# Second attention of a two-layer transformer block: both halves of the scores at the head of a round

## The chip, the core and the metric

The kernel runs on one core of a Trainium2 chip. The metric is the device time of one execution in microseconds (us). Before the change three timed executions gave 514.21, 514.8 and 516.99 us; the median is 514.8 us.

## The reference

The input `x` holds 16 sequences of 128 tokens with 128 features, `ctx_768` holds 16 contexts of 128 rows with 96 features. Four layers follow each other, each added to its own input:

```python
x = x + L0_xattn(layernorm(x), ctx)    # 16 heads of 8, softmax over 128 keys
x = x + L0_ffn(layernorm(x))           # 8 experts, the two best of each token
x = x + L1_xattn(layernorm(x), ctx)    # 16 heads of 64
x = x + L1_ffn(layernorm(x))           # 16 experts, each takes its 32 best tokens
```

The change lies in the third layer, which is

```python
q = split(x @ Wq + lora(x))                             # 16 heads of 64
k, v = split(ctx[:124] @ Wk + ...), split(ctx[:124] @ Wv + ...)
k2, v2 = split(ctx[124:] @ Wk_ipa), split(ctx[124:] @ Wv_ipa)   # the last 4 rows
out = softmax(q k^T / 8) v + softmax(q k2^T / 8) v2
return out @ Wo + bo + lora(out)
```

## The kernel before

All of the work is written out for each engine by hand. An engine takes its instructions in the order of its program, and semaphores, counted up by the engine that makes a value and waited on by the one that takes it, join the engines. Nothing is rearranged by a scheduler. So what sets the order is the text of the five functions called `round1` (one for each of TensorE, VectorE, ScalarE and GpSimd, and weights on SyncE).

The second attention runs in rounds, from -1 to 16. In round `b` the scores and the softmax of sequence `b` are made, while the probabilities of `t = b - 1` are turned and multiplied with the values, and the queries, keys and values of `f = b + 1` are made. A part of the first feed-forward layer, that of sequence `g = b + 4`, runs between them. All 16 heads of one sequence are held at once. Their scores lie in four of the eight banks of PSUM, banks 0 to 3, four heads in each, and banks 4 to 7 serve all the rest in turns.

TensorE's program in an ordinary round `b`, with short names used below:

- S0 is `scores(b, 0)` (L1510), which fills banks 0 and 1, and S1 is `scores(b, 1)`, which fills banks 2 and 3.
- T0 to T3 are `turn(t, n)` (L1521), four transposes each.
- Q0 and Q1 are `queries(f, n)` (L1530), F0 and F1 are the two halves of `ffn(g, ...)` (L1463), both in bank 7.
- K0 and K1 are `keys` (L1538), O0 and O1 are `outputs(t, n)` (L1551), V0 and V1 are `values` (L1558), `inputs` (L1564) turns one tile, and P is the projection (L1721).

The order is S0, T0, Q0, T1, Q1, F0, S1, T2, K0, T3, F1, O0, O1, K1, V0, `inputs`, V1, P. The waits that matter here: Q1 uses the bank of T0 and waits until T0's result is copied, K0 waits likewise for T1's copy, T2 waits for ScalarE's copy of Q0, F1 waits for ScalarE's `weighted` (L1111, F0's result times the expert's weight). O1 reads the copies of T2 and T3 and uses T3's bank, so it waits for T3's copy. S1 waits for the second half of the keys, `Z.k1_sb`, of its own sequence, for which V1 of the round before has waited already.

VectorE's program in round `b`: M0 (`shifted(b, 0)`, L772, L773, L775: the maxima of bank 0), C0 (`turned(t, 0)`, L783: the copy of T0), M1, C1, one reciprocal (L789), then small jobs that differ from round to round (statistics in every round up to 12, parts of the choice of experts in rounds 1 to 8, of the later router in 13 and 14), then M2, C2, M3, a copy of K0 (L919), C3, `weighted` (L745), three reciprocals and the small softmax of the four extra keys. It ends with the residual (L306), which waits for P. In round 15 other copies (`turned` on ScalarE, L1173) and one-hot tiles (`onehot`, L872) for the last layer's gather (L1609 on TensorE, told what to fetch by L1601) come in between.

ScalarE's program in round `b`: the exponentials (`powers`, L1150) of bank 0, the copy of Q0 (L1157), the exponentials of bank 1, the copy of Q1, `weighted` (L1111, four instructions), the exponentials of banks 2 and 3, then copies of O0, K1, O1, the turned tile, V0 and V1. Exponentials of bank `n` wait for M`n`.

The waits of the scores and of the turns, in the code before:

```python
def scores(b, half):
    pe.wait_ge(Z.q_sb, 2 * b + half + 1)
    pe.wait_ge((Z.k0_sb, Z.k1_sb)[half], b + 1)
    pe.wait_ge(Z.ki, b + 1)
    after(pe, Z.exp, CH * (b - 1) + 2 * half + 2)
...
queries(f, 1, *((Z.p_sb, CH * t + 1) if there(t) else (Z.q_sb, 2 * f)))
...
outputs(t, 1, *p_copied(t, 3))
```

Of the kernel before, what the change touches and what calls it, by code (L numbers as in the profile page):

```python
# [37 lines left out]
def after(eng, sem, value):  # L38

    if not isinstance(value, int) or value >= 1:  # L40
        eng.wait_ge(sem, value)


def there(b):
    return not isinstance(b, int) or 0 <= b < B
# [6 lines left out]
def build_program(nc, T, out):  # L52

    with ExitStack() as ctx:
# [15 lines left out]
        def blocks(b_, rows=128):  # L70
            return b_[0:rows, :].rearrange("p (g n) -> p g n", g=CH)
# [1256 lines left out]
        def _(pe):  # L1328
# [132 lines left out]
            def ffn(g, half, to):  # L1461

                pe.matmul(blocks(to), xT0[:, g % 8, :], we[:, 4 * half:4 * half + 4, :], start=True, stop=True)\  # L1463
                    .then_inc((F.ya, F.yb)[half], 1)
# [36 lines left out]
# [6 lines that stand above are left out]
                for c in range(CH):  # L1507
                    for odd in range(2):
                        rows = slice(D1 * odd, D1 * odd + D1)
                        mm = pe.matmul(blocks(bank[2 * half + odd])[:, c, :], q1T[rows, b % 2, CH * half + c, :],  # L1510
                                       k1T[rows, b % 2, CH * half + c, :], start=True, stop=True)
                        if c == CH - 1:
                            mm.then_inc(Z.score, 1)

            def turn(t, n, freed, count):

                pe.wait_ge(Z.norm, CH * t + n + 1)
                pe.wait_ge(Z.ipa_p, t + 1)
                after(pe, freed, count)
                for c in range(CH):  # L1520
                    mm = pe.transpose(blocks(bank[(4, 6, 5, 4)[n]])[:, c, :], p1[:, t % 2, n, c, :], ident[:, :])  # L1521
                mm.then_inc(Z.turned, 1)
# [89 lines left out]
            def round1(b):  # L1612
# [3 lines left out]
                    pe.wait_ge(W.added, ALL_ADDED)  # L1616
                if there(b):
                    scores(b, 0)
                if there(t):
                    turn(t, 0, Z.o_sb, 2 * t)  # L1620
                if b == B:
# [26 lines left out]
                if there(g):  # L1648
                    if j:
                        pe.wait_ge(F.step, HEAD_STEPS * j + 1)  # L1650
                    ffn(g, 0, bank[7])
                if there(b):
                    scores(b, 1)
                if there(t):
                    turn(t, 2, *((Z.q_sb, 2 * f + 1) if there(f) else (Z.v_sb, 2 * B - 1)))
                if b == B:
# [125 lines left out]
            for b in range(-1, B + 1):  # L1782
                round1(b)
# [95 lines left out]
```

## Time and profile before

| what | value |
|---|---|
| median of the timed executions | 514.8 us |
| span of the profiled execution, first to last instruction | 513.1 us |
| TensorE busy | 487.3 us, 95% |
| VectorE busy | 354.2 us, 69% |
| ScalarE busy | 288.2 us, 56% |
| GpSimd busy | 234.4 us, 46% |
| second attention, rounds 0 to 16 | about 135 to 393 us |

The profile gives no other time for the profiled execution than its span. The median lies 1.7 us above it.

The table of rounds is read from the timeline of TensorE and VectorE, in us. A round begins where S0 begins on TensorE. "C0" is the start of VectorE's first copy, counted from the round's start. "J" is the time of the small jobs: from the reciprocal behind C1 until the last small job has given way to the next instruction, without the wait for S1 behind it.

| round | begins | length | C0 | J |
|---|---|---|---|---|
| 1 | 146.56 | 16.81 | 3.04 | 1.95 |
| 2 | 163.37 | 15.25 | 1.94 | 2.03 |
| 3 | 178.62 | 15.61 | 1.95 | 2.49 |
| 4 | 194.23 | 15.68 | 2.47 | 1.96 |
| 5 | 209.91 | 16.64 | 2.41 | 1.96 |
| 6 | 226.55 | 15.26 | 1.95 | 2.03 |
| 7 | 241.81 | 15.60 | 1.94 | 2.49 |
| 8 | 257.41 | 15.23 | 1.95 | 1.96 |
| 9 | 272.64 | 15.24 | 1.95 | 0.67 |
| 10 | 287.88 | 15.61 | 2.39 | 0.68 |
| 11 | 303.49 | 16.29 | 3.08 | 0.67 |
| 12 | 319.78 | 17.68 | 3.07 | 0.66 |
| 13 | 337.46 | 16.16 | 1.95 | 0.68 |
| 14 | 353.62 | 14.35 | 1.94 | 1.18 |
| 15 | 367.97 | 14.84 | 2.13 | |

Rounds 12 and later have no F0 and F1. Rounds 1 and 5 carry two more steps of TensorE, 12 and 13 the router's. In a profile an instruction's row has its start, its duration, engine, line, operation, output and input, and how many it stands for. The duration of a pipelined matmul includes its end, so that the next one can begin before it is over. In brackets stands how long the engine was idle before it, and who ended that.

### The profile page before, as it was taken

The page shows a single profiled execution, that of the slowest core. Times are in us where ns is not written, and L with a number is a line of the kernel's source. Part 1 is how long each engine was busy: PE and PEld are TensorE (multiplying, and loading weights), DVE is VectorE, ACT ScalarE, POOL GpSimd, SP SyncE. Part 2 cuts the span into 40 slices and gives each one's busy share as a digit, 9 for nine tenths or more (in the row PEclk, how much of TensorE's full clock was granted, in tenths as well). Part 3 has the DMA queues.
Part 4 walks back from the last instruction along what each step waited for, and adds up shares of the span by engine and source line. Part 5 has one row for each costly group of instructions (what it writes and reads, how often), then busy time and mean ns, then how long its engine had stood idle before and what let it go on. Part 6 is the DMA issues. An engine that isn't in the chain of part 4 may idle for free.

```text
span 513.1 us, 13570 instructions
## 1 busy us (share of the span) xinstructions
PE 487.3 (95%) x5109; PEld 378.7 (74%) x5113; DVE 354.2 (69%) x1000; ACT 288.2 (56%) x984; POOL 234.4 (46%) x331
## 2 busy tenths in 40 slices
PE   4799999998999999999999999899999999999996
PEld 3466766656668778887787777788757897799995
DVE  5888989766786678566786665757866588535553
ACT  3366566463586776666867657665664444413332
POOL 4845545035365544575444755324231980090440
PEclk9699999999999999999999999999999999999999
DMA  8900000000001100111000000022202100000001
GB/s 229 234 3 4 3 3 3 3 1 8 4 1 32 34 20 16 34 33 34 3 2 2 4 3 3 1 66 64 64 0 71 56 0 1 1 22 24 1 2 42
DMA packets 21872, 14.48 MB, mean 28 GB/s; under 512 B 5928, under 2 KB 21136, under 8 KB 21808
## 3 DMA queue, kind: packets, MB, share of 16 engines
q1 hardware_dynamic: 20704, 13.31, 9.6%
q8 instruction: 42, 0.69, 0.6%
q10 hardware_dynamic: 1104, 0.30, 0.3%
q14 instruction: 22, 0.18, 0.1%
HBM read 12.30 MB, written 1.05 MB: 26 GB/s over the span
## 4 chain that ended last, share of the span: by engine, by line
PE 79%; DVE 12%; ACT 3%; issue 2%; DMA 1%; POOL 1%; ACTq 0%; DVEq 0%; POOLq 0%
PE bank L1792 9%; PE bank L1721 6%; PE bank L1551 5%; PE bank L1558 5%; PE bank L1801 5%; PE bank L1538 5%; PE bank L1510 5%; PE bank L1374 5%; PE bank L1463 5%; PE bank L1521 4%; PE bank L1530 4%; PE bank L1808 3%; PE bank L1609 3%; PE bank L1359 3%; ACT work L1150 2%
## 5 line engine op out<-in xcount | busy, mean ns | idle before, releaser
L1150 ACT ACTIVATE work<-bank,negmax 128x124 f32<-128x124 f32 x256 | 90.0, 387 | 52.2 <-DVE ipa_s L775 52.0
L498 POOL TENSOR_TENSOR work<-work,rsum 128x496 f32<-128x496 f32 x64 | 64.1, 1012 | 120.2 <-DVE rsum L789 120.2
L533 POOL TENSOR_SCALAR work<-work,slot 128x128 f32<-128x128 f32 x64 | 49.7, 792 | 48.3 <-DVE slot L864 29.4
L1150 ACT ACTIVATION_READ_ACCUMULATOR work<-bank,negmax 128x1 f32 x256 | 58.9, 230 | 0.0
L1792 PE MATMUL bank<-work 128*128 128x256 f32 x224 | 53.4, 381 | 0.0
L1014 DVE SCALAR_TENSOR_TENSOR work<-work,bank 128x256 f32<-128x256 f32 x64 | 26.9, 421 | 33.0 <-ACT work L1302 32.8
L1302 ACT ACTIVATE work<-bank 128x256 f32<-128x256 f32 x64 | 24.5, 383 | 40.6 <-PE bank L1792 29.1
L481 POOL TENSOR_TENSOR work<-work 128x512 f32<-128x512 f32 (+2 forms) x48 | 39.2, 817 | 12.1 <-DVE work L745 9.6
L306 DVE TENSOR_TENSOR x_all<-bank,x_all 128x128 f32<-128x128 f32 x16 | 4.7, 292 | 57.4 <-PE bank L1721 55.4
L1792 PEld LDWEIGHTS bank<-work 128*128 128x128 f32 x224 | 40.3, 190 | 4.7 <-DVE work L1017 0.2
L773 DVE TENSOR_REDUCE negmax<-bank 128x4 f32<-128x496 f32 x64 | 42.5, 664 | 0.0
L432 POOL TENSOR_TENSOR rstd<-veps,minus_half 128x1 f32<-128x1 f32 (+3 forms) x28 | 21.2, 755 | 46.1 <-DVE veps L575 45.8
L783 DVE COPY work<-bank 128x512 f32<-128x512 f32 x60 | 40.9, 681 | 0.8 <-PE bank L1521 0.8
L1510 PEld LDWEIGHTS bank<-work 64*128 64x128 f32 x512 | 31.1, 187 | 13.9 <-ACT work L1157 7.6
L629 DVE TENSOR_REDUCE negmax<-bank 128x8 bf16<-128x1024 f32 x32 | 39.1, 1221 | 2.2 <-PE bank L1344 1.7
L1521 PE MATMUL bank<-ident,work 128*128 128x128 f32 x256 | 40.1, 279 | 0.1
L1510 PE MATMUL bank<-work 64*128 64x128 f32 x512 | 37.2, 285 | 1.1 <-issue 1.1
L1090 ACT ACTIVATE work<-bank 128x1024 f32<-128x1024 f32 x32 | 31.0, 1021 | 11.8 <-PE bank L1359 11.8
L1551 PEld LDWEIGHTS bank<-work 128*64 128x64 f32 x512 | 27.7, 136 | 13.5 <-issue 8.7
L1721 PEld LDWEIGHTS bank<-work 128*128 128x128 f32 x256 | 31.1, 192 | 7.4 <-ACT work L1163 5.4
L1530 PE MATMUL bank<-xT,work 128*128 128x128 f32 x256 | 34.3, 278 | 1.6 <-DVE work L783 1.4
L1538 PE MATMUL bank<-cT_all,work 96*128 96x124 f32 x256 | 35.1, 280 | 0.0
(197 smaller groups left out, 1101.1 us busy)
## 6 DMA issues: line engine op xcount, KB each, us to landing
work<-in_L_ffn_w_dram SPq DMA_DIRECT2D x42, 128.0 KB, 2.3
x_all<-in_x_dram SPq DMA_DIRECT2D x4, 256.0 KB, 5.8
out_dram<-x_all SPq DMA_DIRECT2D x4, 256.0 KB, 2.6
ctx_all<-in_ctx_dram SPq DMA_DIRECT2D x4, 192.0 KB, 6.0
ctx_all<-in_L_ffn_w_dram SPq DMA_DIRECT2D x6, 128.0 KB, 2.3
work<-in_L_xattn_Wq_dram SPq DMA_DIRECT2D x1, 512.0 KB, 6.5
work<-in_L_xattn_Wo_dram SPq DMA_DIRECT2D x1, 512.0 KB, 8.2
work<-in_L_ffn_We_dram SPq DMA_DIRECT2D x1, 512.0 KB, 5.7
```

The lines of the kernel that those rows point to most:

```text
L498: pool.tensor_tensor(part, part, rsum1[:, b % 2, CH * n:CH * n + CH].unsqueeze(2).broadcast_to((128, CH, ORG)), ALU.mult).then_inc(Z.norm, 1)
L533: ins = pool.tensor_scalar(ohw_of(e)[:, k, :], count[:, :], slot[:, h, 0, k, e % E1:e % E1 + 1], slot[:, h, 1, k, e % E1:e % E1 + 1], ALU. ...
L773: dve.tensor_reduce(negmax1[:, b % 2, part], got_s[:, :, 0:ORG], X, ALU.max, negate=True)
L783: dve.tensor_copy(p1T[:, CH * n:CH * n + CH, :], blocks(bank[(4, 6, 5, 4)[n]])).then_inc(Z.p_sb, 1)
L1150: ins = act.activation(p1[:, b % 2, n, c, 0:ORG], blocks(bank[n])[:, c, 0:ORG], ACT.Exp, bias=negmax1[:, b % 2, h:h + 1], accum_out=sums1[ ...
L1510: mm = pe.matmul(blocks(bank[2 * half + odd])[:, c, :], q1T[rows, b % 2, CH * half + c, :], k1T[rows, b % 2, CH * half + c, :], start=True ...
L1521: mm = pe.transpose(blocks(bank[(4, 6, 5, 4)[n]])[:, c, :], p1[:, t % 2, n, c, :], ident[:, :])
L1530: mm = pe.matmul(blocks(bank[5 - n])[:, c, :], wq1[:, part], xT[:, f % 2, :], start=True, stop=True)
L1538: mm = pe.matmul(bank[6][:, ORG * c:ORG * c + ORG], wk1[0:C, part], cT_all[:, f, 0:ORG], start=True, stop=True)
L1551: mm = pe.matmul(blocks(bank[5 - n])[D1 * odd:D1 * odd + D1, c, :], v1[:, t % 2, D1 * h:D1 * h + D1], p1T[:, CH * (2 * n + odd) + c, :], s ...
L1721: mm = pe.matmul(bank[7][:, 0:D], o1T[:, c, :], wo1[:, c, :], start=(c == 0), stop=(c == 7))
L1792: mm = pe.matmul(halves(bank[4 + c])[:, n, :], up_weights(e, n, c), xgT[e // E1][:, :, e % E1, :], start=True, stop=True)
```

## The change

One call moves. `scores(b, 1)` is called directly behind `scores(b, 0)`, at the head of TensorE's round, and no longer between `ffn(g, 0)` and `turn(t, 2)`. The work, the banks, the semaphores and the waits within the call are the same. The programs of all other engines are unchanged.

```diff
                 if there(b):
                     scores(b, 0)
+                    scores(b, 1)
                 if there(t):
                     turn(t, 0, Z.o_sb, 2 * t)
...
                     ffn(g, 0, bank[7])
-                if there(b):
-                    scores(b, 1)
                 if there(t):
                     turn(t, 2, *((Z.q_sb, 2 * f + 1) if there(f) else (Z.v_sb, 2 * B - 1)))
```

An ordinary round on TensorE, round 2, from P of the round before (L1721) to O0 and O1. Before:

```order
251 L1721 MATMUL bank<-work 128x128 x8
252 L1510 MATMUL bank<-work 128x128 x8
253 L1521 MATMUL bank<-ident,work 128x128 x4
254 L1530 MATMUL bank<-xT,work 128x128 x4
255 L1521 MATMUL bank<-ident,work 128x128 x4
256 L1530 MATMUL bank<-xT,work 128x128 x4
257 L1463 MATMUL bank<-work 128x512
258 L1510 MATMUL bank<-work 128x128 x8
259 L1521 MATMUL bank<-ident,work 128x128 x4
260 L1538 MATMUL bank<-cT_all,work 128x124 x4
261 L1521 MATMUL bank<-ident,work 128x128 x4
262 L1463 MATMUL bank<-work 128x512
```

The same place after the change (L1721 is L1720 there):

```order
249 L1720 MATMUL bank<-work 128x128 x8
250 L1510 MATMUL bank<-work 128x128 x16
251 L1521 MATMUL bank<-ident,work 128x128 x4
252 L1530 MATMUL bank<-xT,work 128x128 x4
253 L1521 MATMUL bank<-ident,work 128x128 x4
254 L1530 MATMUL bank<-xT,work 128x128 x4
255 L1463 MATMUL bank<-work 128x512
256 L1521 MATMUL bank<-ident,work 128x128 x4
257 L1538 MATMUL bank<-cT_all,work 128x124 x4
258 L1521 MATMUL bank<-ident,work 128x128 x4
259 L1463 MATMUL bank<-work 128x512
```

T0, Q0, T1, Q1 and F0 come eight matmuls later, and everything from T2 on has the same work ahead of it as before.

VectorE's order from C1 of round 2 to M2 and C2, which is the same in both kernels (L310 to L575 are the statistics, L714 and L715 compare the experts):

```order
265 L783 COPY work<-bank 128x512
266 L789 RECIPROCAL rsum<-sums 128x4
267 L310 BN_STATS stats<-x_all 128x6
268 L572 BN_AGGR mv<-stats 128x2
269 L575 TENSOR_SCALAR veps<-mv 128x1
270 L714 TENSOR_TENSOR work<-work 128x256
271 L715 TENSOR_TENSOR work<-work,lower 128x256
272 L772 TENSOR_REDUCE ipa_max<-bank 128x4
273 L773 TENSOR_REDUCE negmax<-bank 128x4
274 L775 TENSOR_TENSOR ipa_s<-bank,ipa_max 128x16
275 L783 COPY work<-bank 128x512
```

Nothing moved there: VectorE still takes the scores of bank 2 only behind both copies and the small jobs.

## Rows read from the trace of the kernel before

**Rows 1.** Waits of TensorE in rounds 2 to 12: total, times, longest.

```profile
PE bank L1551 <- DVE work L783: 1.4, 4, 0.8
PE bank L1530 <- DVE work L783: 1.4, 3, 0.8
```

**Rows 2.** Timeline of TensorE, round 6: start, duration, engine, line, operation, tiles, count.

```profile
226.55 1.16 PE L1510 MATMUL bank<-work 64*128 64x128 f32 x16
227.64 0.66 PE L1521 MATMUL bank<-ident,work 128*128 128x128 f32 x4
...
229.47 1.06 PE L1530 MATMUL bank<-xT,work 128*128 128x128 f32 x8
...
231.31 1.16 PE L1510 MATMUL bank<-work 64*128 64x128 f32 x16
...
234.23 1.02 PE L1463 MATMUL bank<-work 128*128 128x512 f32 x2
235.18 1.99 PE L1551 MATMUL bank<-work 128*64 128x128 f32 x32
237.10 1.16 PE L1538 MATMUL bank<-cT_all,work 96*128 96x124 f32 x8
...
241.81 1.16 PE L1510 MATMUL bank<-work 64*128 64x128 f32 x16
```

**Rows 3.** Timeline of VectorE, round 6.

```profile
227.74 0.17 DVE L772 TENSOR_REDUCE ipa_max<-bank 128x4 f32<-128x16 f32 x1 [0.22 <-PE bank L1510]
...
228.50 0.68 DVE L783 COPY work<-bank 128x512 f32<-128x512 f32 x1
...
230.44 0.17 DVE L789 RECIPROCAL rsum<-sums 128x4 f32<-128x4 f32 x1
...
232.57 0.17 DVE L772 TENSOR_REDUCE ipa_max<-bank 128x4 f32<-128x16 f32 x1
...
235.25 0.68 DVE L783 COPY work<-bank 128x512 f32<-128x512 f32 x1
```

**Rows 4.** Timeline of VectorE, round 3: its first and its last copy.

```profile
180.57 0.68 DVE L783 COPY work<-bank 128x512 f32<-128x512 f32 x1
...
187.67 0.68 DVE L783 COPY work<-bank 128x512 f32<-128x512 f32 x1
```

**Rows 5.** Timeline of TensorE: waits in rounds 0, 3, 11, 14 and 15.

```profile
142.13 1.13 PE L1463 MATMUL bank<-work 128*128 128x512 f32 x2 [0.79 <-ACT work L1111]
...
188.50 1.09 PE L1551 MATMUL bank<-work 128*64 128x128 f32 x16 [0.15 <-DVE work L783]
...
307.39 1.13 PE L1530 MATMUL bank<-xT,work 128*128 128x128 f32 x8 [0.82 <-DVE work L783]
...
362.28 1.09 PE L1551 MATMUL bank<-work 128*64 128x128 f32 x16 [0.66 <-DVE work L783]
...
372.24 1.12 PE L1609 MATMUL bank<-work 128*128 128x512 f32 x2 [0.19 <-DVE work L872]
```

**Rows 6.** Timeline of VectorE, rounds 12, 14 (first and last copy) and 15.

```profile
327.99 0.68 DVE L814 SCALAR_TENSOR_TENSOR work<-work,bank 128x512 f32<-128x512 f32 x1
...
355.56 0.68 DVE L783 COPY work<-bank 128x512 f32<-128x512 f32 x1
...
361.45 0.68 DVE L783 COPY work<-bank 128x512 f32<-128x512 f32 x1
...
370.10 0.68 DVE L783 COPY work<-bank 128x512 f32<-128x512 f32 x1
...
371.44 0.75 DVE L872 TENSOR_SCALAR work<-bank,tok 128x512 f32<-128x512 f32 x1
```

**Rows 7.** Timeline of ScalarE, rounds 0 and 11 (`weighted`) and 12 (the router's tanh).

```profile
140.88 1.20 ACT L1111 ACTIVATE work<-bank,work 128x128 f32<-128x128 f32 x4
...
310.36 1.20 ACT L1111 ACTIVATE work<-bank,work 128x128 f32<-128x128 f32 x4
...
327.12 0.66 ACT L1190 ACTIVATE work<-bank 128x512 f32<-128x512 f32 x1
```

## The prediction

> **What bounds the kernel now.** I read the page's busy shares first: TensorE has matmuls in 95% of the span, no other engine over 69%. The time is therefore TensorE's work and the few holes in it. The move adds and removes no instruction, so only the holes can change. In the waits of TensorE over rounds 2 to 12 [rows 1] there are two that count, both for VectorE's copy L783: the outputs (O1) and the queries (Q1), 1.4 us each. VectorE is thus the engine whose schedule matters, although it is busy for 69% only. Next come the timelines of one round. Round 6 on TensorE [rows 2] runs from 226.55 to 241.81 without a hole, 15.26 us, and S1 starts 4.76 us into it. VectorE in the same round [rows 3] shows the state before the change: M0 begins at 227.74, as soon as S0 is over (226.55 + 1.16), C0 follows at 228.50 without a wait since T0 was over by 228.30, and M2 at 232.57 comes just behind the small jobs and S1's end (232.47).
>
> **What moves.** S0 takes 1.09 us of TensorE before T0 can start [rows 2], and S1 as much. With S1 in front, T0, Q0, T1, Q1 and F0 start 1.09 us later, while T2 and all behind it start as before, the round being as long. No wait of S1 holds it at the head: V1 of the round before has waited for the same keys, and the exponentials of bank 3 are over in the middle of that round. What changes is when VectorE gets its inputs. M0 is unchanged. T0 now starts 2.18 us into a round and is over 0.66 us later; with the 0.03 us from S0's end to M0, C0 can start no earlier than 2.87. Before, it started at 1.94 or 1.95 in rounds 2, 3, 6, 7, 8, 9, 13 and 14 (table of rounds), directly behind M0. VectorE now stands still for 0.92 us there, with M1 behind the copy in its queue although S0 has filled bank 1. M2 in turn can start earlier, since S1 is over at 2.28.
>
> **The rule for one round.** In round 3 C3 started 7.10 us after C0 [rows 4], of which the small jobs J are 2.49; the rest, 4.61, is six pieces of M and C and the copy of K0 at their usual pace. O1 started 0.83 us after C3 [rows 5], 188.50 against 187.67. So afterwards O1 can start no earlier than 2.87 + 4.61 + J + 0.83 = 8.31 + J. TensorE itself is ready for O1 at 9.59 us (O0 starts 8.63 into round 6, and half of the 1.92 until K1 is the first half) [rows 2]. A round stays free of a hole while J is at most 1.28 us. T1's copy needs no more: T1 is over at 2.87 + 1.33, just when M1 is. A round with a hole is 0.07 us longer than the hole itself: round 3 started O1 0.29 late and was 0.36 longer than 15.25.
>
> **Rounds that lose**, J from the table of rounds:
> - 2 and 6, J 2.03: O1 at 10.34, 0.75 late, with 0.07 it is 0.82 each, 1.64 together. They had no hole, but only 0.06 us to spare: C3 at 235.25 plus 0.83 is 236.08, O1 could start at 236.14 [rows 2, 3].
> - 3 and 7, J 2.49: O1 at 10.80, 1.21 late, 1.28 longer than an empty round against 0.36 before: 0.92 each, 1.84 together.
> - 8, J 1.96: O1 at 10.27, 0.68 late: 0.75.
> - 4, J 1.96: the same 0.75, but the round had already lost 0.43 at Q1 (15.68 against 15.25), which goes. Net 0.32.
> - 14, no feed-forward step, so TensorE comes to O1 1.9 us earlier and is waiting already: O1 at 8.66 [rows 5], C3 at 361.45 [rows 6]. Now 8.31 + 1.18 = 9.49: 0.83.
> - 15: C0 started 2.13 in [rows 6], now 2.87. The one-hot tile at 371.44 is queued behind M1, and the gather at 372.24 waited for it [rows 5]. ScalarE's exponentials of bank 1 wait for the same M1, and the next `tell` for ScalarE's copy behind them. Both arms shift by the same 0.74, and I take it in full; if ScalarE's arm had room the round would lose less, down to 0.
>
> Sum of the losses: 1.64 + 1.84 + 0.75 + 0.32 + 0.83 + 0.74 = 6.12 us.
>
> **Rounds that gain.** Where VectorE came late into the round, C0 held Q1 up. Q1 now starts 1.09 us later by itself, at 4.01, and C0, which was later than or near 2.87 anyhow, no longer holds it.
> - 10: 0.36 (15.61 to 15.25).
> - 11: C0 at 3.08, the hole before Q1 at 307.39 [rows 5] made the round 16.29 long. All of 1.04 would go, but then ScalarE is late: its `weighted` starts at 310.36 and F1 can follow 1.25 us behind its start (round 0: 142.13 after 140.88) [rows 5, 7]. That is 311.61, 8.12 into the round, where TensorE is ready for F1 at 7.68 [rows 2]. A hole of 0.44 + 0.07 stays: gain 0.53.
> - 12: VectorE would be earlier by the 1.70 us that it waited for S1, but its product L814 at 327.99 [rows 6] needs the tanh, which ScalarE has at 327.12 + 0.66 = 327.78 [rows 7], with all ScalarE's work before it unmoved. C3 comes 0.18 earlier: gain 0.18.
> - 1: F0 waited some 0.16 us for a copy of the expert's logits, which now has room: gain 0.16, an estimate from the length of that round.
>
> Sum of the gains: 0.36 + 0.53 + 0.18 + 0.16 = 1.23 us.
>
> **Rounds at nothing.** 0 has no turns and its holes are ScalarE's, whose order is the same. 9 has J 0.67, far under 1.28. 5 gets its logits 1.09 later on VectorE, and O1 would wait for C3 until 10.9 where TensorE is ready at 11.0: covered by 0.1, and worth up to 0.3 if not. 13 has 0.7 to spare before O0. In an ordinary round ScalarE's `weighted` starts some 0.45 later since Q0 and M1 are; that leaves F1 about 0.2 us. GpSimd's normalisation moves by at most 0.9 us, and it stood still for 5 us a round.
>
> **The sum.** 6.12 - 1.23 = 4.89 us. The profiled execution's span of 513.1 becomes 518.0; the median lies 1.7 us higher, at 514.8, so it becomes **519.7 us**, 0.95% more.
>
> **A page that says otherwise.** Rows 1 show TensorE, the busiest engine, waiting for VectorE's copies at two places. The Trainium skill, Perfetto Trace Analysis, Optimization Strategy, says to look for the gaps on the most contended engine and to make the things it waits for start sooner or finish faster. Taken by that rule the change is right: the scores for half of VectorE's maxima are there some 3 us before VectorE comes to them. It would change the sum from a loss to the gain of the first rival below. The trace speaks against it, for M2's wait was not what made C3 late; in the crowded rounds M2 had followed the small jobs at once.
>
> **Rivals.**
> - *The earlier scores pay, faster.* VectorE takes M2 up to 1.3 us sooner, and all the holes at L783 close. For it: rounds 9 to 12 show M2 waiting for S1 for over a microsecond. The price is the 1.4 + 1.4 us of rows 1 and some 0.07 for each of seven, 3.3 us: 511.5. It decides at J below 1.28 with C0 not delayed, and eight rounds of the table are above. 5%.
> - *C0's wait is absorbed, no change.* The copy could be held less than 0.92 us, or the pieces between C0 and C3 could run closer together once bank 2 is ready. If only the gains come and round 15's shift vanishes, it is 514.8 - 1.2 = 513.6; that takes all of O1's slack from somewhere the rows don't show. 7%.
> - *Half of it.* Round 15's and 14's shifts hidden by ScalarE, and 0.2 us less in each of rounds 2 to 8: 4.9 - 1.5 - 1.2 = 2.2, 517.0. 15%.
> - *ScalarE becomes late too.* If `weighted` is later by 0.5 more than I find, F1 waits about 0.3 us in rounds 1, 5, 9, 10 and 11, where O1 doesn't cover it, and round 5's 0.1 of cover goes: 4.9 + 1.8 = 6.7, 521.5. For it: 0.2 us is all the room there is. 13%.
> - *The forecast*: 60%.
>
> **The numbers.** The forecast alone spans about 518.3 to 521.0, from seven terms of some 0.1 each and round 15. The half case lies at 517.0 and ScalarE's at 521.5; the range of 516.6 to 522.0 takes in both and leaves out the two first rivals and some tails, under 2 in 10. A measurement of this kernel can tell about 0.5% from no change, 2.6 us here. Slower by more: the forecast, ScalarE's case and a third of the half case, 0.78. Within: 0.17. Faster: 0.05.
>
> **What the profile afterwards would show.** If right: TensorE's busy time unchanged; C0 with an idle time of about 0.9 us before it, ended by TensorE's L1521, in rounds 2, 3, 6, 7, 8, 9 and 14; M2 without any wait for L1510 in any round; TensorE's wait for L783 at L1551 in rounds 2 to 12 up from 1.4 us to about 5, at Q1 gone; rounds 2 and 6 at 16.07, 3 and 7 at 16.53, 8 and 4 at 16.0, 9 at 15.24, 10 at 15.25. It is wrong if C0 follows M0 at once, if C3 in round 2 starts earlier than 9.3 us into the round, if F1 waits for L1111 in ordinary rounds, or if holes appear at the head of a round, before S1.

## The result and the profile after

The changed kernel takes 518.55 us, the median of 15 executions, against 516.17 us for the kernel before in as many on the same chips. The ratio is 1.0046, with a 95% interval from 1.003 to 1.0061: about 2.4 us slower, between 1.5 and 3.1. The forecast was 4.9 us slower, counted from 514.8 us, the median of the first three executions of the kernel before; over 15 executions that median is 516.17. Its sign and mechanism hold, its size is twice the measured one, and the loss lies just under the 0.5% that the text had named as its bound, so the largest chance (0.78 for slower by more than 0.5%) fell on the wrong side of that line, though the interval reaches over it (0.3% to 0.6%).

The profiled execution spans 516.1 us, 3.0 more than before. The second attention begins 1.28 us later in it (136.44 instead of 135.16), and the runs do not put that part down to the change. In the profiled executions of the experiments below it begins at 133.93, 134.84 and 136.46 in kernels that have the call at the head of every round (`e6_after_load`, `e3_vector_order`, `e7_jobs_moved`), at 135.90 and 135.95 in kernels that have it there in none (`e4_behind_turn1`, `e5_before_load`), and at 135.17 and 135.23 in the two that move it in some rounds. The start thus varies by more than 1.28 us whatever the place of the call. The rounds themselves account for the rest. Their lengths, read from one residual (L306, which follows each projection by 0.10 us) to the next, and for round 1 from the starts of S0:

| round | before | after | difference | forecast |
|---|---|---|---|---|
| 1 | 16.81 | 16.32 | -0.49 | -0.16 |
| 2 | 15.26 | 15.90 | +0.64 | +0.82 |
| 3 | 15.60 | 16.35 | +0.75 | +0.92 |
| 4 | 15.68 | 15.80 | +0.12 | +0.32 |
| 5 | 16.65 | 16.32 | -0.33 | 0 |
| 6 | 15.25 | 15.89 | +0.64 | +0.82 |
| 7 | 15.61 | 16.35 | +0.74 | +0.92 |
| 8 | 15.23 | 15.81 | +0.58 | +0.75 |
| 9 | 15.23 | 14.88 | -0.35 | 0 |
| 10 | 15.62 | 15.10 | -0.52 | -0.36 |
| 11 | 16.29 | 15.67 | -0.62 | -0.53 |
| 12 | 17.68 | 17.31 | -0.37 | -0.18 |
| 13 | 16.21 | 16.05 | -0.16 | 0 |
| 14 | 14.30 | 14.93 | +0.63 | +0.83 |
| 15 | 14.93 | 15.43 | +0.50 | +0.74 |
| sum | | | +1.76 | +4.89 |

The rounds give 1.8 us and the medians 2.4. The interval covers both; where the 0.6 us between them lies is not known.

The waits of TensorE in the same rounds as [rows 1], and those of VectorE in rounds 2 to 15, both of the kernel after (who waited, for whom; total, times, longest):

```profile
PE bank L1551 <- DVE work L783: 7.1, 10, 1.2
PE bank L1463 <- ACT work L1111: 0.3, 1, 0.3
```

```profile
DVE work L783 <- PE bank L1521: 7.1, 13, 0.8
...
DVE ipa_max L772 <- PE bank L1510: 1.3, 7, 0.2
```

The 1.4 us at Q1 in [rows 1] are gone and the 1.4 at the outputs have become 7.1. Of these, 5.1 us lie in rounds 2 to 4 and 6 to 8, which got longer, and 2.0 are the two holes of round 12, which made up 1.1 us of the 1.4 before. VectorE, which before waited 8.5 us for scores (L772) in rounds 2 to 15 and 0.6 for turns, now waits 7.1 us for turns. The 1.3 us that it still waits for scores are all M0's; M2 waits in no round. Round 3 shows both ends of that. VectorE first, then TensorE, kernel after:

```profile
181.24 0.17 DVE L772 TENSOR_REDUCE ipa_max<-bank 128x4 f32<-128x16 f32 x1 [0.19 <-PE bank L1510]
182.73 0.69 DVE L783 COPY work<-bank 128x512 f32<-128x512 f32 x1 [0.65 <-PE bank L1521]
...
187.17 0.17 DVE L772 TENSOR_REDUCE ipa_max<-bank 128x4 f32<-128x16 f32 x1
...
189.84 0.68 DVE L783 COPY work<-bank 128x512 f32<-128x512 f32 x1
```

```profile
188.75 1.09 PE L1551 MATMUL bank<-work 128*64 128x128 f32 x16 [0.35 <-DVE work L783]
190.67 1.09 PE L1551 MATMUL bank<-work 128*64 128x128 f32 x16 [0.83 <-DVE work L783]
```

The round begins at 180.05. C0 starts 2.68 us in, after standing still, where it started at 1.95 [rows 4]. From C0 to C3 it is 7.11 us (7.10 before), from C3 to O1 0.83. O0 follows C2, which starts at 187.92, by the same 0.83 us and so waits too. M2 at 187.17 follows the small jobs without a wait, and the scores it reads had been there since about 182.1.

Round 9, which has few small jobs, shows what the forecast had missed. TensorE, kernel before:

```profile
272.64 1.16 PE L1510 MATMUL bank<-work 64*128 64x128 f32 x16
273.74 0.66 PE L1521 MATMUL bank<-ident,work 128*128 128x128 f32 x4
...
276.45 1.02 PE L1463 MATMUL bank<-work 128*128 128x512 f32 x2
277.41 1.16 PE L1510 MATMUL bank<-work 64*128 64x128 f32 x16
278.50 0.66 PE L1521 MATMUL bank<-ident,work 128*128 128x128 f32 x4
278.99 1.05 PE L1538 MATMUL bank<-cT_all,work 96*128 96x124 f32 x8
```

Kernel after:

```profile
276.57 2.06 PE L1510 MATMUL bank<-work 64*128 64x128 f32 x32
278.56 0.66 PE L1521 MATMUL bank<-ident,work 128*128 128x128 f32 x4
...
281.27 1.02 PE L1463 MATMUL bank<-work 128*128 128x512 f32 x2
282.13 0.60 PE L1521 MATMUL bank<-ident,work 128*128 128x128 f32 x4
282.57 1.05 PE L1538 MATMUL bank<-cT_all,work 96*128 96x124 f32 x8
...
284.85 1.97 PE L1551 MATMUL bank<-work 128*64 128x128 f32 x32
```

From S0 to T0 the two halves take 1.99 us, where apart they took 1.10 and 1.09. F0 gives way to T2 after 0.86, where it gave way to S1 after 0.96, and T2 to K0 after 0.44, not 0.49. Together that is 0.20 + 0.10 + 0.05 = 0.35 us in a round in which no work changed.

### The profile page after: what moved, and what is told of

Same layout as the page of the kernel before. It is cut to its first block, busy times and chain, and to the rows that moved or that the text cites. A ratio compares the mean times of both kernels' runs of the same rounds, so it can differ in the third digit from the quotient of the medians.

```text
span 516.1 us, 13574 instructions
## 1 busy us (share of the span) xinstructions
PE 484.1 (94%) x5113; PEld 378.6 (73%) x5113; DVE 354.6 (69%) x1000; ACT 289.8 (56%) x984; POOL 234.4 (45%) x331
## 3 DMA queue, kind: packets, MB, share of 16 engines
HBM read 12.30 MB, written 1.05 MB: 26 GB/s over the span
## 4 chain that ended last, share of the span: by engine, by line
PE 74%; DVE 16%; ACT 4%; issue 2%; DMA 1%; ACTq 1%; POOL 1%; DVEq 0%; POOLq 0%
PE bank L1791 9%; PE bank L1720 6%; PE bank L1558 5%; PE bank L1510 5%; PE bank L1800 5%; PE bank L1374 5%; PE bank L1551 5%; PE bank L1538 4%; DVE work L783 4%; PE bank L1521 3%; PE bank L1807 3%; PE bank L1463 3%; PE bank L1609 3%; PE bank L1359 3%; ACT work L1150 2%
## 5 line engine op out<-in xcount | busy, mean ns | idle before, releaser
L1150 ACT ACTIVATION_READ_ACCUMULATOR work<-bank,negmax 128x1 f32 x256 | 60.2, 235 | 0.0
L306 DVE TENSOR_TENSOR x_all<-bank,x_all 128x128 f32<-128x128 f32 x16 | 4.7, 292 | 57.3 <-PE bank L1720 55.2
L1551 PE MATMUL bank<-work 128*64 128x128 f32 x512 | 33.9, 277 | 8.4 <-DVE work L783 8.4
L1521 PEld LDWEIGHTS bank<-ident,work 128*128 128x128 f32 x256 | 29.5, 141 | 10.3 <-issue 7.3
L1720 PEld LDWEIGHTS bank<-work 128*128 128x128 f32 x256 | 31.1, 191 | 7.4 <-ACT work L1163 5.4
L1463 PE MATMUL bank<-work 128*128 128x512 f32 x64 | 33.1, 605 | 1.5 <-ACT work L1111 1.5
```

The lines of the kernel that those rows point to most:

```text
L1150: ins = act.activation(p1[:, b % 2, n, c, 0:ORG], blocks(bank[n])[:, c, 0:ORG], ACT.Exp, bias=negmax1[:, b % 2, h:h + 1], accum_out=sums1[ ...
L1551: mm = pe.matmul(blocks(bank[5 - n])[D1 * odd:D1 * odd + D1, c, :], v1[:, t % 2, D1 * h:D1 * h + D1], p1T[:, CH * (2 * n + odd) + c, :], s ...
L1720: mm = pe.matmul(bank[7][:, 0:D], o1T[:, c, :], wo1[:, c, :], start=(c == 0), stop=(c == 7))
```

## Experiments

**The move in seven rounds only.** `e1_gainers`:

```diff
                 if there(b):
                     scores(b, 0)
-                    scores(b, 1)
+                if there(b) and (b in (1, 5, 9, 10, 11, 12, 13)):
+                    scores(b, 1)
...
+                if there(b) and not (b in (1, 5, 9, 10, 11, 12, 13)):
+                    scores(b, 1)
                 if there(t):
                     turn(t, 2, ...)
```

> The move is made only in rounds 1, 5 and 9 to 13, the rest is as before. Theory (each round by itself: VectorE's first copy C0 can start no earlier than the turn, and a round loses only if its small jobs J on VectorE are long): these seven rounds keep the lengths they have in the changed kernel, 0.32 (round 5), 0.49 (1), 0.35 (9), 0.52 (10), 0.62 (11), 0.36 (12) and 0.18 us (13) shorter than before, all others stay as before: 2.8 us less than before, ratio 0.9945. Rival (the loss is not one of single rounds: the second attention of the changed kernel starts 1.3 us later, and that comes with the move): its start moves by 1.3 us here too, the ratio is 0.997 or above.

Measured: 513.54 us against 516.23, ratio 0.9949 (0.993 to 0.9967). All rounds fit the forecast within 0.02 us, those with the move as in the changed kernel (5: 16.32, 9: 14.88, 10: 15.10, 11: 15.67, 13: 16.04), the others as before (2: 15.26, 3: 15.60, 14: 14.30), except round 12, which was 18.87 us long in the profiled execution and not 17.31. The section began at 135.17. So the length of a round goes by the place of the call in that round and not in its neighbours, and this kernel has the gains without the late start. Round 12 is a matter of TensorE's clock. TensorE's timeline and the busy times of 328.7 to 332.5 (columns: stretch, its length, busy time of TensorE, its weight loads, VectorE, ScalarE and GpSimd, granted clock, share and rate of DMA):

```profile
326.78 1.09 PE L1551 MATMUL bank<-work 128*64 128x128 f32 x16 [1.18 <-DVE work L783]
328.70 1.97 PE L1551 MATMUL bank<-work 128*64 128x128 f32 x16 [0.83 <-DVE work L783]
330.60 1.12 PE L1570 MATMUL bank<-ident,work 128*128 128x128 f32 x4
```

```profile
328.70:332.50 3.80, 3.80 (x27) 3.47 (x28) 0.84 (x5) 1.43 (x5) 3.78 (x6) 0.56 0.05 9
```

The second half of the outputs took 1.97 us where it takes 1.09, behind two holes of 1.18 and 0.83 us. The granted clock is 0.56 on average over that stretch: it was 1.00 up to 328.35, inside the second hole, 0.50 from 328.70 to 331.50 and 1.00 again from 332.10 on. That is a fall from full speed, 2.4 GHz, to the lower level, 1.2 GHz, and back. The changed kernel has the same two holes in round 12 and no fall in its profiled execution.

**The complement.** `e2_losers` is the same edit with `b in (2, 3, 4, 6, 7, 8, 14, 15)`.

> The complement: the move is made only in rounds 2, 3, 4, 6, 7, 8, 14 and 15. Theory: these rounds are longer than before by 0.64, 0.74, 0.12, 0.64, 0.75, 0.57, 0.65 and 0.50 us, as in the changed kernel, all others as before: 4.6 us more than before, ratio 1.009. Rival (late start): the start of the second attention, and not these rounds, carries 1.3 us, the ratio is 1.003 to 1.006 as for the whole change.

Measured: 521.31 us against 516.23, ratio 1.0104 (1.0077 to 1.0131). Rounds 2, 3, 4, 6, 7, 8, 14 and 15 are 15.90, 16.35, 15.80, 15.89, 16.35, 15.81, 14.94 and 15.43 us long. The others are as before within 0.02 us, except round 5 (16.71 instead of 16.65), and the section starts at 135.23. Rounds 2 to 16 take 234.25 us against 229.56: 4.7 more. The move is worth -2.7 us in seven rounds and +5.1 in eight by the medians, together +2.4, which is the whole change as timed (by the table of rounds -2.8 and +4.6, together +1.8). The rival of a late start has fallen with both.

**VectorE's order made to fit.** `e3_vector_order`, on the changed kernel:

```diff
                 if there(b):
                     shifted(b, 0)
+                    shifted(b, 1)
                 if there(t):
                     turned(t, 0)
...
                 if there(b):
-                    shifted(b, 1)
+                    shifted(b, 2)
                 if there(t):
                     turned(t, 1)
...
-                if there(b):
-                    shifted(b, 2)
                 if b == 12:
                     hidden(0)
```

> The changed kernel, with VectorE's order made to fit: M0, M1, C0, M2, C1, small jobs, C2, M3 instead of M0, C0, M1, C1, small jobs, M2, C2, M3. Theory (the loss is VectorE standing still before C0): M1 fills the 0.73 us, C0 starts at about 2.7 us without a wait, C3 at 6.56 + J. Rounds 2 and 6 fall to about 15.15, 3 and 7 to 15.6, 8 to 15.05, 9 stays at 14.9; in 10 and 11 C0 is later by M1 and some of the gain before Q1 goes; round 15 may lose up to 0.6 since its one-hot tile comes behind M2. Together 2 to 3 us less than before, ratio 0.995. Rival (the loss is the turn's copies being late for their readers whatever VectorE does in between): no gain over the changed kernel, ratio 1.004 or above.

Measured: 514.04 us against 516.23, ratio 0.9956 (0.993 to 0.9981). Rounds 2, 3, 4, 6, 7, 8 and 9: 15.15, 15.61, 15.58, 15.16, 15.60, 15.07 and 14.88, as forecast. Rounds 10 and 11 did not lose their gain (15.12, 15.67), against what I had expected there; round 15 lost 0.21 and not up to 0.6. Round 12 was 19.00 us long with a granted clock of 0.55 over 3.7 us. VectorE in round 3 (which begins at 177.72):

```profile
178.91 0.17 DVE L772 TENSOR_REDUCE ipa_max<-bank 128x4 f32<-128x16 f32 x1 [0.18 <-PE bank L1509]
179.66 0.17 DVE L772 TENSOR_REDUCE ipa_max<-bank 128x4 f32<-128x16 f32 x1
180.41 0.68 DVE L783 COPY work<-bank 128x512 f32<-128x512 f32 x1
...
186.76 0.68 DVE L783 COPY work<-bank 128x512 f32<-128x512 f32 x1
```

The copy still starts 2.69 us into the round, as in the changed kernel, but M1 stands ahead of it and nothing is lost: C3 comes at 9.04, not 9.79. So in this round the late turn in itself costs nothing. What cost was the order of VectorE's queue, which kept it idle with M1's and M2's scores waiting in PSUM.

**The second scores behind T1.** `e4_behind_turn1`, on the kernel before:

```diff
                     turn(t, 1, Z.v_sb, 2 * min(f, B))
+                if there(b):
+                    scores(b, 1)
...
-                if there(b):
-                    scores(b, 1)
                 if there(t):
                     turn(t, 2, ...)
```

> The kernel before, with the second half of the scores moved behind the turn of group 1, between T1 and Q1, so that no turn that VectorE copies early is delayed, and Q1 still starts 1.1 us later. Theory: C0 at 1.95 as before, no loss in rounds 2, 6, 8 (15.1 to 15.25), 3 and 7 at 15.6, 14 as before, and the holes before Q1 in rounds 4, 10 and 11 close: 2 us or more less than before, ratio 0.996. Round 9 tells the changes of shape apart: 14.9 if TensorE is faster because S1 no longer stands behind the wide F0, about 15.1 if half of it comes from S0 and S1 being together. Rival (the second scores must be late for ScalarE's sake): ratio 1.0 or above.

Measured: 514.39 us against 516.23, ratio 0.9969 (0.9952 to 0.9986). Rounds 10, 11 and 12 at 15.27, 15.69 and 17.33, round 3 at 15.60, 14 at 14.20: the holes before Q1 close and no round loses 0.1 us but 5 (16.75). Round 9 is 15.28, as long as before. TensorE in it:

```profile
273.29 1.16 PE L1510 MATMUL bank<-work 64*128 64x128 f32 x16
274.39 0.65 PE L1521 MATMUL bank<-ident,work 128*128 128x128 f32 x4
...
275.77 0.60 PE L1521 MATMUL bank<-ident,work 128*128 128x128 f32 x4
276.30 1.16 PE L1510 MATMUL bank<-work 64*128 64x128 f32 x16
277.39 1.16 PE L1530 MATMUL bank<-xT,work 128*128 128x128 f32 x8
278.39 1.02 PE L1463 MATMUL bank<-work 128*128 128x512 f32 x2
```

T1 gives way to S1 after 0.53 us where it gave way to Q1 after 0.44, S1 takes its 1.09 again, and Q1 gives way to F0 after 1.00 instead of 0.89. F0 gives way to T2 after 0.86 here as well, but what is won there is paid back at T1 and at Q1. The 0.35 us of round 9 are therefore not won by taking S1 away from behind the wide F0; they come with S0 and S1 standing together. Both guesses for round 9 (14.9 and about 15.1) were too low.

**The threshold of the small jobs.** Two more maxima on VectorE in rounds 9 and 10, once on each kernel; their results go nowhere. `e5_before_load` and `e6_after_load`:

```diff
                 dve.wait_ge(Z.turned, CH * t + n + 1)
+                if n == 1 and t in (8, 9):
+                    for again in range(2):
+                        dve.tensor_reduce(more[:, 2 * (t - 8) + again, :], blocks(bank[6]), X, ALU.max)
                 dve.tensor_copy(p1T[...], ...)
```

> The kernel before, with two more maxima of 0.60 us each on VectorE between M1 and C1 in rounds 9 and 10 (their results go nowhere), so that the jobs between C0 and C3 grow by 1.2 us to about 1.9. Theory: O1 may start at C0 + 4.61 + 1.87 + 0.83, which is 9.26 us into round 9 and 9.7 into round 10, before TensorE is ready for it (9.59 and 9.96). Both rounds keep their length, 15.23 and 15.62. Rival (any work added to VectorE shows, wherever C0 stands): about 1 us more in each.

> The changed kernel with the same two maxima of 0.60 us in rounds 9 and 10. Theory: C0 at 2.68 makes O1 possible at 9.99 us, where TensorE is ready at 9.24 now. Round 9 goes from 14.88 to about 15.7, round 10 from 15.10 to about 15.7. Rival (the threshold in J is no real one, rounds 2 to 8 lose for another reason): no difference to the same load in the kernel before, that is, lengths unchanged.

Measured on the kernel before: rounds 9 and 10 at 15.23 and 15.61, unchanged. Measured on the changed kernel: 15.72 and 15.71 instead of 14.88 and 15.10. (One execution was timed for each, 517.22 and 518.41 us, and says nothing more.) VectorE in round 9 with the load, changed kernel, and the hole that it made on TensorE:

```profile
278.13 0.69 DVE L787 COPY work<-bank 128x512 f32<-128x512 f32 x1 [0.65 <-PE bank L1525]
...
279.49 1.28 DVE L786 TENSOR_REDUCE more<-bank 128x4 f32<-128x512 f32 x2
...
284.61 0.68 DVE L787 COPY work<-bank 128x512 f32<-128x512 f32 x1
```

```profile
285.44 1.09 PE L1555 MATMUL bank<-work 128*64 128x128 f32 x16 [0.55 <-DVE work L787]
```

C3 starts 6.48 us after C0 (278.13), which is 4.61 + 0.67 + 1.20, and O1 0.83 behind it. The same 1.2 us are free where C0 starts at 1.95 and cost 0.84 where it starts at 2.68. So there is a limit on J, as the forecast has it. Where it lies the runs show only roughly: 0.67 us is free and 1.87 is not. Worked out from the rows of round 9 it is about 1.1 us (an estimate: TensorE is ready for O1 at 9.24, and 2.68 + 4.61 + 0.83 is 8.12).

**The small jobs out of the way.** `e7_jobs_moved`, on the changed kernel:

```diff
-                if b in (4, 8):
-                    head_shares((b + 4) // 4)
                 if there(b + 3) and b >= 0:
                     ffn_statistics(b + 3)
-                if b in (2, 6):
-                    head_ties()
-                if b in (3, 7):
-                    head_beats()
...
                     ipa_norm(b)
+                if b in (2, 6):
+                    head_ties()
+                if b in (3, 7):
+                    head_beats()
+                    head_shares((b + 5) // 4)
```

> The changed kernel, with the choice of experts taken out of J: the steps of rounds 2, 3 and 4 (6, 7 and 8) go to the end of VectorE's rounds 2 and 3 (6 and 7), where it waits for P for over 4 us. J is then about 0.67 in all of rounds 2 to 11. Theory: rounds 2, 3, 6, 7 and 8 fall from 15.90, 16.35, 15.89, 16.35 and 15.81 to 14.9, round 4 from 15.80 to about 15.0, 14 and 15 keep their loss: 4.9 us less than before, ratio 0.990. Rival (those rounds lose by something else that comes with the move, or the jobs' cost only comes back at the round's end): they stay over 15.5, ratio above 0.998.

Measured: 510.95 us against 515.97, ratio 0.9905 (0.9883 to 0.9926). Rounds 2, 6, 7 and 8: 14.94, 14.94, 14.88 and 14.83. Rounds 3 and 4 together take 30.38 us (31.28 before, 32.15 after), half a microsecond more than I had expected. By the starts of the projection on TensorE round 3 takes 14.88 us, as forecast, and round 4 takes 15.56. In round 4 the residual (L306) starts 0.52 us into the round instead of 0.11. With a normalisation (L698) between it and M0, as in the changed kernel, C0 starts at 2.85 instead of 2.68, and F1 waits 0.31 us for ScalarE's `weighted`. The moved jobs themselves were over at 193.57, 0.37 us before the round began; what held the residual is open. The same five rounds that lost 0.6 to 0.75 us by the move now gain 0.3 to 0.7 us on the kernel before, with TensorE's order that of the changed kernel. No run moves the jobs on the kernel before, so how much of the 5.0 us they would give without the earlier scores is not measured. Round 9 gives a hint: with few small jobs it takes 15.23 us in the kernel before and 14.88 with the move.

**And the last holes.** `e8_jobs_and_late_hidden` is `e7_jobs_moved` with the old place of the second scores in rounds 14 and 15, and

```diff
-                if b == 12:
-                    hidden(0)
                 if there(t):
                     turned(t, 2)
...
                 if there(t):
                     turned(t, 3)
+                if b == 12:
+                    hidden(0)
```

> As e7_jobs_moved, with the second scores in their old place in rounds 14 and 15, and in round 12 VectorE's product for the router (L814) behind C3 instead of ahead of C2, so that no copy waits for ScalarE's tanh. Theory: 14 and 15 are back at 14.3 and 14.93, round 12 falls from 17.3 by about 1.8 us since O0 and O1 find their copies, and its two holes of 1.2 and 0.8 us go, behind which the granted clock fell to half for some 3.4 us in two earlier profiles (round 12 18.9 and 19.0 us long). 7.8 us less than before, ratio 0.985. Rival (the tanh's wait moves to the next step that needs the product, the second turn of the router): round 12 stays over 17, ratio 0.988.

Measured: 508.49 us against 515.97, ratio 0.9864 (0.9835 to 0.9894), the fastest of all: 7.5 us less than before. Round 12 is 15.52 us long (17.68 before), 14 and 15 are 14.30 and 14.91. TensorE's waits in rounds 2 to 12:

```profile
PE bank L1462 <- ACT work L1110: 0.6, 2, 0.3
PE bank L1550 <- DVE work L783: 0.3, 1, 0.3
```

Of the 2.8 us of [rows 1] 0.3 are left; the 0.6 us for ScalarE at F1 are new.

## Why the forecast was right in kind and twice too large

- **The rule for one round held.** C3 - C0 = 4.61 + J and O1 - C3 = 0.83 came out within 0.02 us, in rounds 2 to 4, 6 to 8 and 14 of the changed kernel and under load. The rounds that lose are the eight that the text named, for the reason it gave. That the hole at O1 takes the place of M2's wait is shown by `e3_vector_order`, by the threshold in `e5_before_load` and `e6_after_load`, and by `e7_jobs_moved`.
- **The step that failed** is "T2 and all behind it start as before, the round being as long", and with it "S1 as much" as S0. TensorE's order was taken as a sum of fixed pieces. Put together, the two halves take 1.99 us and not 2.18, and the round's own work is 0.35 us shorter (round 9: 15.23 to 14.88). C0's earliest start is therefore 2.68 and not 2.87, 0.19 less, which is about what each of the eight losing rounds came out shorter than forecast (0.17 to 0.24 us, 1.5 in all). The other seven gain 0.1 to 0.35 us more than the text had, 1.6 in all. 4.89 - 1.5 - 1.6 is the measured 1.8 us of the rounds. The rest of the spans' difference, 1.28 us, lies ahead of the section.
- **Luck.** The time itself, 519.7 us forecast and 518.55 measured, looks closer than the change was. The forecast counted from 514.8 us where 15 executions give 516.17, and that makes up for 1.4 of the 2.5 us by which the change was overestimated.
- **Gains**: Q1's holes in rounds 4, 10 and 11 closed, and F1 kept one for ScalarE in round 11 (0.31 us in the waits above, 0.44 in the forecast). Round 12's hole for the tanh stayed.
- **Round 15** lost 0.50 and not 0.74. The mechanism held: with C0 at 2.68 and not 2.87 its delay is 0.55 us, the first one-hot tile starts 0.56 later in the round, and TensorE's wait for it rose from 0.19 us [rows 5] to 1.10. ScalarE's arm moved by 0.51, counted at the next `tell` (L1601).
- **Rivals.** The faster one did not happen: the scores came earlier and VectorE did not take them. The Trainium skill, Perfetto Trace Analysis, Optimization Strategy, says to make what the gaps wait for start sooner or finish faster. By that rule the copies were the thing to be made earlier, and `e3_vector_order` and `e7_jobs_moved` do that and gain (2.2 and 5.0 us). The absorbed wait did not happen either: C0 stood still for 0.65 us, and the way from C0 to C3 did not shrink (7.11 us in round 3 against 7.10). The half case had the size (517.0 forecast, +2.2 us) but not the reason. "F1 late in ordinary rounds" was not seen.

## What to carry to other kernels

When work is moved ahead on one engine, follow the queue of the engine that takes it: the early result is worth nothing if that engine's next instruction waits for something the move has delayed. Look there for the slack of each round separately; the same move gained 2.7 us in seven rounds and lost 5.1 in eight, and light rounds told nothing about loaded ones. Then rearrange the second queue as well. Here another order of VectorE's maxima turned the loss of 2.4 us into a gain of 2.2, moving its small jobs into one of 5.0; with two rounds put back and round 12's product moved as well it was 7.5.

## What the hardware showed that was not expected

- **Two groups of scores take less of TensorE together than apart.** Their matmuls are 64 rows deep, those of their neighbours 96 or 128. A half takes 1.09 or 1.10 us between such neighbours, two halves together 1.99; T1 gives way to S1 after 0.53 and to Q1 after 0.44. In a round this is 0.35 us. That the change of shape is what costs, up to 0.1 us each time, fits all of these rows but was not tested by itself.
- **The clock can fall behind short holes.** In round 12 of two profiled executions (`e1_gainers`, `e3_vector_order`) the granted clock was 0.55 to 0.56 over the 3.7 or 3.8 us behind two holes of about 1.1 and 0.8 us, and the round was 1.6 to 1.7 us longer than in the changed kernel, which has the same holes and kept its clock. `e6_after_load` and `e7_jobs_moved` have those holes and kept it too. At the start of the section it fell in `e5_before_load` and `e6_after_load`: 0.59 over 135.90 to 139.50 in the one and 0.65 over 133.90 to 137.50 in the other, behind a hole of 1.06 and 1.05 us. The kernel before has that hole of 1.06 us too and takes 1.09 us for the half behind it, at full speed. So the fall does not go by the length of these holes alone; what else decides it is open. `e8_jobs_and_late_hidden` has no such holes in that round.
